# A message-passing layer: loads released by the count of issued scatter pairs, and the search for duplicate rows moved to ScalarE

## The reference, cut to what matters

```python
row, col = edge_index[0], edge_index[1]                     # src, dst
tp = fctp_messages(node_features[col], edge_attr_tensor, W1, W2, W3, W4)
messages = tp @ Wm + bm
agg = jax.ops.segment_sum(messages, row, num_segments=N_NODES)
upd = jnp.concatenate([node_features, agg], axis=-1) @ Wu + bu
# returned: layernorm(x + (node_features + upd))
```

## Time and profile before

| | |
|---|---|
| median of three executions | 1829.69 us |
| the profiled execution | 1834.27 us |
| its span on the core | 1832.5 us, granted clock of TensorE 0.957 of full speed |
| busy in the span | PE 1581.1 us (86%), DVE 1594.1 (87%), POOL 1067.6 (58%), ACT 900.5 (49%) |
| mean rate of the DMAs | 267 GB/s, 490.07 MB |
| chain that ended last | DMA 33%, issue 21%, PE 18%, DVE 14%, POOL 9%; scatters' landings alone 18% |

### The profile page before, as it was taken

The page is one execution under the profiler, slowest core; times in us unless marked ns, Lnnn a source line. Parts: engine busy times, 40 slices in busy tenths (PEclk is TensorE's granted clock), DMA queues, the critical chain, the costliest instruction groups (busy, mean ns, idle before and its releaser), DMA issues.

```text
span 1832.5 us, 35242 instructions
## 1 busy us (share of the span) xinstructions
PE 1581.1 (86%) x11572; PEld 876.3 (48%) x11572; DVE 1594.1 (87%) x1825; ACT 900.5 (49%) x1721; POOL 1067.6 (58%) x837
## 2 busy tenths in 40 slices
PE   4167899999999999999999999999999999298882
PEld 2033444545444554545544454445554454276662
DVE  6276699999999999999999999999999996199994
ACT  1123444545444444555544444445554445088885
POOL 3005777777767777776777777767777774211110
PEclk8688999999999999999999999999999999699996
DMA  9996678888888888888888888888888885899994
GB/s 378 404 395 178 157 234 248 245 244 244 256 244 247 246 247 255 256 247 244 249 255 248 243 250 256 248 242 246 246 252 249 255 248 139 287 391 421 416 418 170
DMA packets 174618, 490.07 MB, mean 267 GB/s; under 512 B 48664, under 2 KB 99096, under 8 KB 149484
## 3 DMA queue, kind: packets, MB, share of 16 engines
q1 hardware_dynamic: 91980, 379.42, 57.5%
q0 software_dynamic: 82304, 109.12, 27.2%
q10 hardware_dynamic: 288, 0.95, 0.2%
HBM read 393.10 MB, written 96.31 MB: 267 GB/s over the span
## 4 chain that ended last, share of the span: by engine, by line
DMA 33%; issue 21%; PE 18%; DVE 14%; POOL 9%; ACT 2%; SPq 1%; POOLq 1%; DVEq 0%; ACTq 0%
DMA agg<-summed,row_idx 18%; DVE prod L527 7%; POOL agg L344 6%; DMA agg<-start_rows 5%; DMA prod<-agg 5%; DMA e_sb<-in_e_rep 4%; PE ps L671 4%; PE ps L678 3%; POOL xg L326 3%; PE ps L659 2%; DVE prod L596 2%; DVE prod L515 2%; DVE stats L615 2%; PE ps L733 1%; PE ps L722 1%
## 5 line engine op out<-in xcount | busy, mean ns | idle before, releaser
L344 POOL DMA_INDIRECT agg<-summed,row_idx x392 | 625.4, 1595 | 363.7 <-DMA agg<-summed,row_idx 183.2
L527 DVE TENSOR_TENSOR prod<-ps,e_sb 128x2048 f32<-128x2048 f32 x294 | 655.3, 2285 | 68.3 <-DMA e_sb<-in_e_rep 47.5
L678 PE MATMUL ps<-prod,packed_sb 128*32 128x512 f32 x2744 | 672.4, 607 | 0.8 <-ACT S_sb L398 0.8
L326 POOL DMA_INDIRECT xg<-in_x_rows,dst_sb x392 | 415.7, 1060 | 187.7 <-issue 113.6
L671 PE MATMUL ps<-prod,packed_sb 128*32 128x512 f32 x2352 | 396.3, 603 | 0.0
L535 DVE TENSOR_TENSOR prod<-ps,e_sb 128x3072 f32<-128x3072 f32 x98 | 328.3, 3350 | 0.0
L515 DVE TENSOR_TENSOR prod<-ps,e_sb 128x2048 f32<-128x2048 f32 x98 | 223.8, 2283 | 49.8 <-issue 32.0
L659 PEld LDWEIGHTS ps<-packed_sb,spread 128*128 128x128 f32 x1176 | 127.8, 143 | 221.8 <-issue 104.5
L441 ACT ACTIVATE summed<-ps 128x644 f32<-128x644 f32 x98 | 69.4, 708 | 330.9 <-PE ps L736 234.0
L659 PE MATMUL ps<-packed_sb,spread 128*128 128x128 f32 x1176 | 174.5, 286 | 51.3 <-issue 28.4
L468 ACT ACTIVATE prod<-prod,shift_n,rstd 128x160 f32<-128x160 f32 (+1 forms) x392 | 166.6, 507 | 40.8 <-DVE shift_n L608 40.8
(11 more groups left out here) (62 smaller groups left out, 1702.4 us busy)
## 6 DMA issues: line engine op xcount, KB each, us to landing
e_sb<-in_e_rep SPq DMA_DIRECT2D x98, 1536.0 KB
e_sb<-in_e_rep SPq DMA_DIRECT2D x98, 1024.0 KB
agg<-start_rows SPq DMA_DIRECT2D x49, 640.0 KB, 15.1
prod<-agg SPq DMA_DIRECT2D x48, 640.0 KB, 10.3
out<-prod POOLq DMA_DIRECT2D x48, 640.0 KB, 7.7
row_sb<-in_src_row SPq DMA_DIRECT2D x98, 256.0 KB
prod<-in_x_t SPq DMA_DIRECT2D x25, 640.0 KB, 12.0
e_sb<-in_x_t SPq DMA_DIRECT2D x24, 640.0 KB, 12.7
```

The costliest lines, as they stand in the source:

```text
L326: nc.gpsimd.indirect_dma_start(xg[g[1] % 2][:, q, :], None, x_rows, bass.IndirectOffsetOnAxis(dst_sb[g[1]][:, q:q + 1].bitcast(U32), 0)).t ...
L344: nc.gpsimd.indirect_dma_start(agg, bass.IndirectOffsetOnAxis(row_idx[g[1]][:, q:q + 1].bitcast(U32), 0), summed[g[1]][:, q // 2, q % 2 * ...
L527: nc.vector.tensor_tensor(prod[g[1] % 2][:, 4 + 4 * i:8 + 4 * i, :].rearrange("p (a b) e -> p a b e", b=2), ps[:, t_bank(g, 1 + i), :].uns ...
L678: return nc.tensor.matmul(ps[32 * quarter:32 * quarter + 32, S_BANK, :], w[:, 32 * half:32 * half + 32], prod[g[1] % 2][:, tile, :], start ...
```

## The change

SP's two attribute loads wait on a new semaphore `pairs_issued`, which POOL raises by one behind the second scatter of each pair, and no longer on landings. `scattered_a` and `scattered_b` become one semaphore, with the same waits on POOL, ACT and DVE. The first 16 `xT` loads no longer wait together for all rounds: their homes are taken in the order `e_sb[0]`, `e_sb[1]`, `prod[1]`, each kind waits for its last reader, and two or three of them are released by each of the last seven counts of issued pairs. ACT finds the trash rows: a Sign of the doubled weight less the weight column (`find_alone`), and two multiplications by the negated trash numbers (`find_trash`) into one of four buffers; DVE keeps the one operation that takes the larger.

```diff
--- before.py
+++ after.py
@@ -31,7 +31,7 @@
 SET_ROWS = 8
 EPS = 1e-5
 
-PACKED = {"ident": P, "eye4": NV, "sum": NV, "trash": TILES, "dup": 2, "w1": 4 * NS, "w2": 2 * NS, "w3": P,
+PACKED = {"ident": P, "eye4": NV, "sum": NV, "trash": 2, "dup": 2, "w1": 4 * NS, "w2": 2 * NS, "w3": P,
           "w4": 2 * NV, "wux_a": D, "wux_b": D}
 
 
@@ -119,7 +119,8 @@
         met = two("met", [P, 2, P], BF16)
         msg = two("msg", [P, TILES, MW])
         summed = four("summed", [P, 2, 2 * MW])
-        moved = sb("moved", [P, TILES])
+        alone = sb("alone", [P, TILES])
+        trash = four("trash", [P, TILES])
         row_idx = four("row_idx", [P, TILES], I32)
 
         stage = prod[0][:, :, :].rearrange("p n e -> p (n e)")
@@ -131,9 +132,9 @@
         NB = GN * D // P
         an = [nodes[:, b * NB:(b + 1) * NB] for b in range(AGG_BUFS)]
         yn = [nodes[:, (AGG_BUFS + b) * NB:(AGG_BUFS + b + 1) * NB] for b in range(Y_BUFS)]
-        homes = [prod[1][:, :, :], e_sb[0][:, :, :], e_sb[1][:, :, :]]
+        homes = [e_sb[0][:, :, :], e_sb[1][:, :, :], prod[1][:, :, :]]
         xT = [home.rearrange("p n e -> p (n e)")[:, b * NB:(b + 1) * NB]
-              for home, count in zip(homes, (8, 4, 4)) for b in range(count)]
+              for home, count in zip(homes, (4, 4, 8)) for b in range(count)]
         assert len(xT) == AHEAD
         stats = two("stats", [P, NODES_A, 6])
         mv = two("mv", [P, NODES_A, 2])
@@ -159,9 +160,8 @@
         es_in = [sem(f"es_in{u}") for u in range(M1)]
         ev_in = [sem(f"ev_in{u}") for u in range(M1)]
         x_gathered = [sem(f"x_gathered{u}") for u in range(M1)]
-
-        scattered_a = sem("scattered_a")
-        scattered_b = sem("scattered_b")
+        scattered = sem("scattered")
+        pairs_issued = sem("pairs_issued")
         xT_in = [sem(f"xT_in{b}") for b in range(AHEAD)]
         agg_in = [sem(f"agg_in{b}") for b in range(AGG_BUFS)]
         nodes_out = [sem(f"nodes_out{b}") for b in range(Y_BUFS)]
@@ -186,6 +186,8 @@
         same_done = sem("same_done")
         msg_copied = sem("msg_copied")
         summed_copied = sem("summed_copied")
+        alone_found = sem("alone_found")
+        trash_found = sem("trash_found")
         std_done = sem("std_done")
         normed = sem("normed")
 
@@ -193,7 +195,7 @@
         wc_copied = sem("wc_copied")
         multiplied = sem("multiplied")
         parts_added = sem("parts_added")
-        idx_step = sem("idx_step")
+        rows_found = sem("rows_found")
         added = sem("added")
         stats_done = sem("stats_done")
         mv_done = sem("mv_done")
@@ -203,7 +205,7 @@
         CONSTS = 2
         PIECES = (n_rows // P + SET_ROWS - 1) // SET_ROWS
         PIECES_OUT = 6
-        DVE_SETUP = 9
+        DVE_SETUP = 8
 
         def hold(engine, passed):
             engine.sem_inc(passed, 1)
@@ -219,7 +221,7 @@
                     hold(sp, sp_passed)
                 if at_least(g, 10):
 
-                    sp.wait_ge(scattered_a, number(g) * 32 - 5 * 32 + 32)
+                    sp.wait_ge(pairs_issued, number(g) * 2 - 5 * 2 + 2)
                     hold(sp, sp_passed)
                 sp.dma_start(e_sb[g[1] % 2][:, 0:4, :], e_rep[number(g), :, 0:4, :].unsqueeze(0).to_broadcast([32, 4, 4, GE])
                              ).then_inc(es_in[g[1]], 16)
@@ -230,7 +232,7 @@
                     hold(sp, sp_passed)
                 if at_least(g, 9):
 
-                    sp.wait_ge(scattered_a, number(g) * 32 - 4 * 32 + 16)
+                    sp.wait_ge(pairs_issued, number(g) * 2 - 4 * 2 + 1)
                     hold(sp, sp_passed)
                 sp.dma_start(e_sb[g[1] % 2][:, 4:ET, :], e_rep[number(g), :, 4:ET, :].unsqueeze(0).to_broadcast([32, 4, ET - 4, GE])
                              ).then_inc(ev_in[g[1]], 16)
@@ -242,7 +244,7 @@
 
             def load_src(g):
                 if at_least(g, 4):
-                    sp.wait_ge(idx_step, number(g) * 2 - 6)
+                    sp.wait_ge(rows_found, number(g) - 3)
                     hold(sp, sp_passed)
                     sp.wait_ge(apart_done, number(g) - 3)
                 sp.dma_start(src_sb[g[1]][:, :], src_idx[number(g), :, :]).then_inc(src_in[g[1]], 16)
@@ -298,12 +300,19 @@
                              ).then_inc(agg_in[n % AGG_BUFS], 16)
 
 
-            sp.wait_ge(rounds, ROUNDS * n_groups)
             for n in range(AHEAD):
+                if n == 0:
+                    sp.wait_ge(multiplied, USES * (n_groups - 1))
+                if n == 4:
+                    sp.wait_ge(multiplied, USES * n_groups)
+                if n == 8:
+
+                    sp.wait_ge(rounds, ROUNDS * n_groups)
+                if n in (0, 2, 4, 6, 8, 10, 13):
+                    sp.wait_ge(pairs_issued, 2 * n_groups - 6 + min(n // 2, 6))
                 load_xT(n)
 
-            sp.wait_ge(scattered_a, 32 * n_groups)
-            sp.wait_ge(scattered_b, 32 * n_groups)
+            sp.wait_ge(scattered, 16 * TILES * n_groups)
             def ahead(n):
 
                 return min(AHEAD + (n_out - AHEAD) * n // (n_out - 4), n_out)
@@ -331,20 +340,20 @@
             def scatter(g, q):
                 if q == 0:
                     pool.wait_ge(summed_copied, number(g) + 1)
-                    pool.wait_ge(idx_step, number(g) * 2 + 2)
+                    pool.wait_ge(rows_found, number(g) + 1)
                 if q % 2 == 0:
 
                     if at_least(g, 1) or q:
-                        pool.wait_ge(scattered_a, number(g) * 32 + q * 8)
-                        pool.wait_ge(scattered_b, number(g) * 32 + q * 8)
+                        pool.wait_ge(scattered, number(g) * 64 + q * 16)
                     else:
                         for u in range(PIECES_OUT):
                             pool.wait_ge(table_set[u], 16 * ((PIECES - u + PIECES_OUT - 1) // PIECES_OUT))
                     hold(pool, pool_passed)
                 nc.gpsimd.indirect_dma_start(
                     agg, bass.IndirectOffsetOnAxis(row_idx[g[1]][:, q:q + 1].bitcast(U32), 0),
-                    summed[g[1]][:, q // 2, q % 2 * MW:q % 2 * MW + D], None, compute_op=ALU.add
-                ).then_inc(scattered_b if q % 2 else scattered_a, 16)
+                    summed[g[1]][:, q // 2, q % 2 * MW:q % 2 * MW + D], None, compute_op=ALU.add).then_inc(scattered, 16)
+                if q % 2:
+                    pool.sem_inc(pairs_issued, 1)
 
             def slot(s):
                 live = lambda d: not isinstance(s[0], int) or 0 <= number(s) + d < n_groups
@@ -436,9 +445,24 @@
             def copy_summed(g):
                 act.wait_ge(summed_ready, number(g) + 1)
                 if at_least(g, 4):
-                    act.wait_ge(scattered_a, number(g) * 32 - 96)
-                    act.wait_ge(scattered_b, number(g) * 32 - 96)
+                    act.wait_ge(scattered, number(g) * 64 - 192)
                 nc.scalar.activation(summed[g[1]][:, :, :], msg_ps, ACT.Copy).then_inc(summed_copied, 1)
+
+            def find_alone(g):
+
+                act.wait_ge(summed_copied, number(g) + 1)
+                if at_least(g, 1):
+                    act.wait_ge(trash_found, number(g) * 2)
+                nc.scalar.activation(alone[:, :].rearrange("p (a b) -> p a b", a=2), summed[g[1]][:, :, D:2 * MW:MW],
+                                     ACT.Sign, bias=dup_sb[:, 1:2], scale=-1.0).then_inc(alone_found, 1)
+
+            def find_trash(g):
+                act.wait_ge(alone_found, number(g) + 1)
+                if at_least(g, 4):
+                    act.wait_ge(rows_found, number(g) - 3)
+                for b in range(2):
+                    nc.scalar.activation(trash[g[1]][:, b:TILES:2], alone[:, b:TILES:2], ACT.Copy,
+                                         scale=trash_sb[:, b:b + 1]).then_inc(trash_found, 1)
 
             def slot(s):
                 live = lambda d: not isinstance(s[0], int) or 0 <= number(s) + d < n_groups
@@ -457,6 +481,8 @@
                     copy_A(shift(s, 1))
                 if live(-2):
                     copy_summed(shift(s, -2))
+                    find_alone(shift(s, -2))
+                    find_trash(shift(s, -2))
 
             run_slots(act, slot, -1, n_groups + 2, 8, (n_groups - 1) // M1 * M1)
 
@@ -503,8 +529,6 @@
             dve.wait_ge(wc_ready, 1)
             nc.vector.tensor_copy(wc_s[:, :], ps[:, M_BANK, 0:D]).then_inc(wc_copied, 1)
             nc.vector.tensor_copy(wc_v[:, :], ps[0:97, M_BANK + 1, 0:D]).then_inc(wc_copied, 1)
-            dve.wait_ge(setup_done, DVE_SETUP - 1)
-            nc.vector.memset(moved[:, :], 0.0).then_inc(setup_done, 1)
 
             def times_xs(g):
                 dve.wait_ge(A_copied, number(g) + 1)
@@ -548,25 +572,14 @@
                     total, more = prod[g[1] % 2][:, 6, :], prod[g[1] % 2][:, 14, :]
                 nc.vector.tensor_tensor(total, total, more, ALU.add).then_inc(parts_added, 1)
 
-            def rows(g, step):
-                n = number(g)
```

(26 more changed lines are left out.)

## The result

| | before | after |
|---|---|---|
| median (runs) | 1829.74 us (4) | 2093.60 us (4) |
| lowest and highest | 1829.28 to 1835.72 | 2089.84 to 2095.68 |
| profiled execution, its span | 1834.27, 1832.5 us | 2095.68, 2093.9 us |
| granted clock of TensorE, mean | 0.957 | 0.915 |

The changed kernel takes 1.1431 times as long (95% interval 1.1402 to 1.146): 264 us more. The forecast was 1764 us with a range of 1746 to 1803, and it was wrong in size and in sign.

The account below looks back on a forecast made before the run. DVE's 14.49 us slot, with a serial load-scatter loop as long, was taken as the bound. Slots 54, start 3 and drain 9 us sum to 66 us less: 1768 for the profiled execution, 1764 us by the median, range 1746 to 1803.

Parts of the forecast that it names:

- What bounds the kernel: Attribute stage: DVE's work sets 14.49 us per slot, late loads add 0.30; the serial load-scatter loop is as long.
- Loads released by issue: Attribute loads go out 1.7 us earlier, behind both scatters; delay between nothing (taken) and a whole load before the second scatter.
- Rival two: Attribute stage: the released load cuts in before the second scatter, slot 15.6 us, 1895 us in all; chance 0.06.
- The rule that speaks against it: DMA engines: taking turns between queues by packet, a released load could come between two waiting scatters, giving 1895 us.
- VectorE's floor: DVE in the attribute stage: one row operation less saves 0.41 us, a floor of 14.08 us per slot.
- ScalarE's three operations: ACT before the copy of S: 1.5 us (0.6 to 2.4) hidden in a 1.94 us gap, costed at nothing.
- Rival three: ACT: Sign needs its own function table, two 1.28 us loads per slot, 1846 us in all; chance 0.03.
- What is late next: POOL needs 13.0 us per slot, PE follows to about 14.0; 0.07 us of stalls kept, slot 14.15 us.
- Start: First loads after the gates act, from group 9: each 1.7 us earlier, 3 us less in all (0 to 8).
- Drain: Last scatters: 13.2 us of contention gone, less 0.6 (0.1 per pair) and 3.4 lost; net 9 us less (4 to 13).
- Rivals one and four: Attribute stage. One: landing wait only moves to POOL, 1797 us, chance 0.15. Four: earlier release unused, 1820, chance 0.04.
- the slots' term: Steady attribute stage: 85 slots go from 14.79 to 14.15 us each, 54 us less, at most 60.

Follow-up runs that it names:

- the engine's count: The changed kernel with the count raised by a memset that GpSimd executes behind each pair's second scatter, not by its queue: 1787.47 us, again 1796.47 us.

## Why the prediction was wrong, step by step

**What bounds the kernel: right.** The serial loop of loads and scatters sets the slot. The new rows under the old gates show it: 0.6 us less in the shortest slot, and a mean slot of 14.84.

**Loads released by issue: the step that failed.** What failed is the time at which the count goes up. The prediction read "The counter goes up once the second scatter of a pair is issued, at 813.14 + 1.58 = 814.72". The program text says so; the queue does not. The increment came 0.2 us after the *first* scatter's start, which on the prediction's rows would be 811.5 and not 814.72: 3.2 us earlier. That "the scatters then are ahead in every queue" was the reason for taking the lower bound, and it fell with it: the slot grew from 14.79 to 17.68 us where 14.15 was forecast. With a count from the engine, the premise holds, and so does what was built on it: the load goes out 1.85 us behind the second scatter's start, and POOL hardly waits for landings. The prediction named no row for the time of the increment and put no price on its coming early. The trace of the kernel before had such a row. `hold` is the same kind of increment; the one of the next gathers stands behind both scatters of a pair in the program. The kernel before, queue and engine:

```profile
L209 POOLq EVENT_SEMAPHORE  x1: 43/43/43, 1024.9 to 1024.9; - x1
```

```profile
1024.54 1.61 POOL L344 DMA_INDIRECT agg<-summed,row_idx  x1 [0.95 <-issue]
1026.46 1.58 POOL L344 DMA_INDIRECT agg<-summed,row_idx  x1 [0.31 <-ACT summed L441]
```

The increment at 1024.9 is 0.4 us behind the first scatter's start and 1.6 us ahead of the second's. Two pairs of other slots, at 1039.83 and 1054.74, have theirs at 1040.3 and 1055.1. So the time of the increment could be read before the change was made.

**Rival two had the mechanism, and too small a size.** It let one load cut in before the second scatter once per slot, for 15.6 us a slot, with a chance of 0.06. In the changed kernel both loads of a slot cut in, and before both scatters of a pair. By its own arithmetic, 13.0 us and both loads, (1.0 + 1.5) MB at 397 GB/s = 6.3 us, would have been 19.3; measured 17.68, because the 13.0 of issuing and the loads overlap in part: two gathers are issued while the load moves (from 1010.73 to 1013.04). Its sign for being right was pairs over 10 us apart; they are 8.84, all of them slowed, where it had one pair of two.

**The rule that speaks against it: neither reading held as put.** The prediction weighed first come, first served against the Trainium skill (DMA: Bandwidth & Descriptors, Queues, rings and completion order), by which a DMA engine takes turns between its queues a packet at a time. In the rows above the load has 3 us to itself, 121 packets against none, although POOL was done with the first scatter at 1008.54: while the load's large packets move, no turns are seen; beside the six-row loads POOL's queue has 7 to 25 packets, where a scatter alone in the drain has 144. From 1012 to 1013 both queues have packets, side by side. But that scatter, by its 2.1 us, would have been there with the load or a tenth of a microsecond ahead of it, so that first come, first served isn't shown either. Either way the loss follows once the load is in front; what decided was when it is issued.

**VectorE's floor: under-sized.** 0.41 us predicted, for a floor of 14.08. The shortest slot went from 14.48 to 13.86 and 13.87, 0.6 us. From the start of the first multiplication to that of line 527 it was 2.89 us, and is 2.37 with the new rows (1000.92 to 1003.29): 0.52 of the 0.6 lie there. Of all this only 0.1 to 0.2 us shows in the mean even with loads in time.

**ScalarE's three operations: right to be hidden, sized on the dear side.** From the ACT rows of after, in order of time:

```profile
1014.84 0.71 ACT L449 ACTIVATE summed<-ps 128x644 f32<-128x644 f32 x1 [3.44 <-PE ps L748]
1015.58 0.30 ACT L456 ACTIVATE alone<-summed,packed_sb 128x4 f32<-128x4 f32 x1
1015.91 0.48 ACT L464 ACTIVATE trash<-alone,packed_sb 128x2 f32<-128x2 f32 x2
1017.46 0.60 ACT L407 ACTIVATE S_sb<-ps 128x512 f32<-128x512 f32 x1 [1.07 <-PE ps L690]
```

From 1015.55 to 1016.39 are 0.84 us (predicted 1.5, between 0.6 and 2.4), and 1.07 us of the gap are left. Rival three is out: there are two loads of a function table in all, as before, and no more.

**What is late next: too hopeful.** PE "can follow down to about 14.0", says the prediction. With the loads in time, the slots are mostly 13.9 us for the first dozen and then mostly 14.5 to 14.6; the mean is 14.30 to 14.42, and in the steady stretch DVE's waits are above all for PE, as the rows of the engine's count show. PE is busy for 388 of the 400 us from 1000 to 1400 there, at a granted clock of 1.00 (the level of 2.4 GHz).

So even with its premise fulfilled, the term would have been 85 x (14.79 - 14.4) = 33 us, not 54. What on PE sets 14.4 was not taken apart.

**Start:** predicted 3 us less, measured 1.2 more; with the engine's count 0.9 more and 0.8 less. Nothing to be had there. **Drain:** predicted 9 us less, measured 11.7 more, in two parts. The last pair of scatters starts 69.3 us behind the last first multiplication, against 60.8 before: nine pairs are left at that point and not eight, and with the gates alone and the old loads it is 69.8, so this part comes from the slots. Behind the last pair's start it takes 12.5 us in place of 9.4, 3.1 more, for which the prediction had put 3.4. What failed of the term's own is the 0.1 us per pair: with the staged loads released by the queue's count, pairs are 7.9 and 9.6 us apart (starts at 1828.16, 1836.01 and 1845.58), and in the run with the new drain alone the last pair starts 60.8 us behind, as before. Where the premise was fulfilled, by the engine's count, the drain is 5.1 and 9.2 us shorter than before, of which 1.4 also come with the old loads.

**Node stage:** predicted nothing; 2.3 us more. It takes 235.1 to 236.6 us in all nine traces with the new rows, and 233.5 to 234.1 in all four with the old ones, so it comes with the new rows; by what way is open.

**Rivals one and four** didn't occur; with the engine's count, landings are waited for 45.0 us in all, not above 183, and the slot is not DVE's old 14.49 either.

With the count in the right place the kernel comes to 1787.47 and 1796.47: inside the range, but 23 and 32 us above the forecast, because the slots' term is 33 us and the start's is nothing. So the prediction, of the kernel that the change describes and not of the one that it makes, was too hopeful of that one as well.
